# Local attention in six layers: dividing the probabilities before their transposition, and a product with the values that comes out transposed

## The reference

```python
def local_attention(q, k, v):
    ...
    bk2, bv2 = (look(bk), look(bv))      # each window sees the one before and itself: 128 keys
    ...
    sim = jnp.einsum('bhwie,bhwje->bhwij', bq, bk2) * QK_SCALE
    sim = jnp.where(mask, -jnp.finfo(sim.dtype).max, sim)
    attn = jax.nn.softmax(sim, -1)
    out = jnp.einsum('bhwij,bhwje->bhwie', attn, bv2)
    return out.reshape(b, h, n, d)
```

## Time and profile before

| | |
|---|---|
| median of 3 runs | 5177.25 us (5173.41 to 5180.86) |
| profiled execution: span from first to last instruction | 5182.7 us |
| PE busy | 4823.6 us, 93% |
| DVE busy | 3429.4 us, 66% |
| ACT busy | 3112.6 us, 60% |
| POOL busy | 2409.7 us, 46% |
| mean granted TensorE clock | 0.978 |

### The profile page before, as it was taken

How to read it: one execution, slowest core, us unless ns; L and a number is a source line. 1 busy time by engine, 2 the same in 40 slices (tenths; PEclk the granted TensorE clock), 3 DMA queues, 4 the chain that set the end, 5 groups by cost and what they waited for, 6 DMA issues and landing times.

```text
span 5182.7 us, 92467 instructions
## 1 busy us (share of the span) xinstructions
PE 4823.6 (93%) x35414; PEld 3013.7 (58%) x35480; DVE 3429.4 (66%) x6514; ACT 3112.6 (60%) x6618; POOL 2409.7 (46%) x2314
## 2 busy tenths in 40 slices
PE   6898999989899898969999999999999999999998
PEld 2232333334334343227877777777777777777776
DVE  4766566676675857757766666666666666666664
ACT  3565555434344444547777677776777677777763
POOL 3211101111011111129777677676767677776762
PEclk8999999999999899989999999999999999999998
DMA  5233222322312222311000000000000000000000
GB/s 121 52 56 59 54 44 55 65 50 48 61 37 50 46 57 43 56 30 46 8 18 26 16 24 20 22 22 20 22 18 24 18 28 16 24 19 19 24 22 21
DMA packets 125161, 188.97 MB, mean 36 GB/s; under 512 B 18896, under 2 KB 67664, under 8 KB 124496
## 3 DMA queue, kind: packets, MB, share of 16 engines
q1 hardware_dynamic: 124720, 183.06, 15.9%
HBM read 150.09 MB, written 32.51 MB: 35 GB/s over the span
## 4 chain that ended last, share of the span: by engine, by line
PE 64%; DVE 14%; ACT 8%; POOL 7%; issue 6%; DMA 1%; SPq 0%; DVEq 0%; POOLq 0%; ACTq 0%
PE psum L1253 16%; PE psum L1300 10%; PE psum L467 4%; PE psum L432 4%; PE psum L453 4%; DVE maxes L655 3%; PE psum L1308 3%; PE psum L1341 3%; PE psum L1332 2%; PE psum L414 2%; PE psum L1323 2%; POOL stats L1633 2%; PE psum L476 2%; ACT probs L836 2%; PE psum L422 1%
## 5 line engine op out<-in xcount | busy, mean ns | idle before, releaser
L836 ACT ACTIVATE probs<-psum 128x1024 f32<-128x1024 f32 x768 | 772.2, 1019 | 609.9 <-PE psum L453 337.7
L655 DVE TENSOR_REDUCE maxes<-psum 128x1 f32<-128x1024 f32 x512 | 616.5, 1212 | 246.6 <-PE psum L432 242.5
L1633 POOL TENSOR_TENSOR stats<-stats,minus_half 128x8 f32<-128x8 f32 x384 | 651.8, 1697 | 32.0
L1439 DVE TENSOR_TENSOR lwork<-psum,rotary 128x512 f32<-128x512 f32 x384 | 264.2, 688 | 513.1 <-PE psum L1300 446.9
L1573 ACT ACTIVATE lprobs<-psum,small_stats,stats 128x128 f32<-128x128 f32 x1536 | 581.1, 474 | 12.3 <-DVE small_stats L1457 11.5
L1629 POOL TENSOR_TENSOR lwork<-lwork 128x512 f32<-128x512 f32 x384 | 493.9, 1286 | 202.9 <-DVE lwork L1441 202.7
L1300 PE MATMUL psum<-wqkv_hi,xs_hi 128*128 128x512 f32 (+1 forms) x1536 | 554.6, 361 | 33.6 <-POOL xs_lo L1620 17.1
L453 PE MATMUL psum<-stack 98*128 98x512 bf16 x1536 | 513.1, 390 | 72.1 <-DVE maxes L655 32.0
L432 PE MATMUL psum<-stack 96*128 96x512 bf16 x1536 | 473.2, 391 | 64.2 <-ACT probs L836 53.1
L1300 PE MATMUL psum<-wqkv_hi,xs_lo 128*128 128x512 f32 (+1 forms) x1536 | 519.6, 338 | 0.0
L1300 PE MATMUL psum<-wqkv_lo,xs_hi 128*128 128x512 f32 (+1 forms) x1536 | 519.3, 338 | 0.0
(11 more groups left out here) (225 smaller groups left out, 11526.7 us busy)
## 6 DMA issues: line engine op xcount, KB each, us to landing
stack<-k_parts SPq DMA_DIRECT2D x288, 128.0 KB
staged<-in_quads SPq DMA_DIRECT2D x144, 256.0 KB, 3.0
k_parts<-parts SPq DMA_DIRECT2D x48, 384.0 KB, 2.9
stack<-q_parts SPq DMA_DIRECT2D x288, 64.0 KB
staged<-in_w SPq DMA_DIRECT2D x54, 256.0 KB, 2.7
ctx<-in_ctxT SPq DMA_DIRECT2D x24, 512.0 KB, 4.7
q_parts<-parts SPq DMA_DIRECT2D x24, 384.0 KB, 2.3
arena<-in_ctxT SPq DMA_DIRECT2D x8, 512.0 KB, 4.8
```

The source lines that it names most:

```text
L655: ins = vector.tensor_reduce(to, pair(("M", u)), AX.XY, ALU.max)
L836: scalar.activation(probs[:, i % 6, :, :], pair(("E", u)), ACT.Exp).then_inc(S_["E_act"], 1)
L1439: vector.tensor_tensor(v4(t1), v4(qk), bc(rotary[:, d % 2, 0, tt], 2, 4), ALU.mult)
L1633: pool_step(gpsimd.tensor_tensor(st[:, 8:16], st[:, 0:8], minus_half[:, :], ALU.pow))
```

## The change

The probabilities are divided by their sums while queries are still on the partitions, in a new stage `dv`, and the product with the values is made the other way round, so that it comes out with features on the partitions, as the output projection wants it. The stage `ot` and the buffer `heads_out` go.

- ACT's exponentials give their sum over the 128 keys as a second output (`accum_out`).
- `dv` (lag 5): DVE takes the reciprocal of the four sums and multiplies the 128x512 probabilities in place, in SBUF.
- `pt` moves from lag 5 to 6 and waits for `dv`; `pv` from 6 to 7.
- `pv`: the values (128 keys x 64 features of a head) are the stationary side, the transposed probabilities (64 queries) the moving one; two heads share the partitions. ACT copies to `att_hi` and DVE subtracts to `att_lo` straight from that bank.
- `vals`, `mixed_vals` and `lprobs` get one slot more, and lose the column of ones; `mixed_vals` is set to 0 at the start and `vals` no longer set. `x_back` gets no buffer of its own: it lies in the rotary tables' first buffer and its load waits for the last use of that.

```diff
-        for stage, lag in (("qkv", 0), ("rot", 1), ("tr", 3), ("sc", 4), ("ex", 4), ("pt", 5), ("pv", 6), ("ot", 7)):
+        for stage, lag in (("qkv", 0), ("rot", 1), ("tr", 3), ("sc", 4), ("ex", 4), ("dv", 5), ("pt", 6), ("pv", 7)):
...
-    rank = {st: i for i, st in enumerate(("wo", "sc", "tr", "rot", "ot", "pv", "ex", "pt"))}
+    rank = {st: i for i, st in enumerate(("wo", "sc", "tr", "rot", "pv", "dv", "ex", "pt"))}
...
-        vals, mixed = psb("vals", [P, 6, 4, LHD + 1]), psb("mixed_vals", [P, 7, 4, LHD + 1])
+        vals, mixed = psb("vals", [P, 7, 4, LHD]), psb("mixed_vals", [P, 8, 4, LHD])
...
-        probs = psb("lprobs", [P, 2, 4, P])
+        probs = psb("lprobs", [P, 3, 4, P])
...
-        heads_out = psb("heads_out", [P, 2, 4, LHD])
...
-        back = psb("x_back", [P, C, S])
+        back = rotary[:, DEPTH % 2].rearrange("p i t s d -> p (i t s d)").rearrange("p (c n) -> p c n", c=C)
...
                 elif stage == "pt":
-                    PE.wait_ge(S_["ex_act"], at_("ex", u))
+                    PE.wait_ge(S_["dv_dve"], at_("dv", u))
...
-                    for h in range(4):
+                    for pair in range(2):
                         for w in range(2):
-                            ins = tensor.matmul(bank(("pv", u, 0))[64 * w:64 * w + 64, h * (LHD + 1):(h + 1) * (LHD + 1)],
-                                                pt[:, h, 64 * w:64 * w + 64], (va if w else vm)[:, h, :], start=True, stop=True)
+                            for e in range(2):
+                                ins = tensor.matmul(bank(("pv", u, 0))[64 * e:64 * e + 64, pair * P + 64 * w:pair * P + 64 * w + 64],
+                                                    (va if w else vm)[:, 2 * pair + e, :], pt[:, 2 * pair + e, 64 * w:64 * w + 64],
+                                                    start=True, stop=True)
                     ins.then_inc(S_["pv_pe"], 1)
-                elif stage == "ot":
-                    PE.wait_ge(S_["pv_dve"], at_("pv", u))
-                    left(one, ("ot", u, 0), PE)
-                    o = heads_out[:, out_at["o", u][0], :, :].rearrange("p (j e) d -> p j (e d)", j=2)
-                    for pair in range(2):
-                        ins = tensor.transpose(bank(("ot", u, 0))[:, tok(pair)], o[:, pair, :], ident[:, :])
-                    ins.then_inc(S_["ot_pe"], 1)
...
+                elif stage == "dv":
+                    pr, rc = probs[:, prob_at["p", u][0], :, :], soft(u)[:, 8:12]
+                    V.wait_ge(S_["ex_act"], at_("ex", u))
+                    step(vector.reciprocal(rc, soft(u)[:, 0:4]))
+                    step.join()
+                    vector.tensor_tensor(pr, pr, bc(rc, 2, P), ALU.mult).then_inc(S_["dv_dve"], 1)
                 elif stage == "pv":
-                    ps = bank(("pv", u, 0))[:, 0:4 * (LHD + 1)].rearrange("p (h d) -> p h d", h=4)
-                    rc = soft(u)[:, 8:12]
-                    V.wait_ge(S_["pv_pe"], at_("pv", u))
-                    left(out_at, ("o", u), V)
-                    step(vector.reciprocal(rc.rearrange("p (h d) -> p h d", d=1), ps[:, :, LHD:LHD + 1]))
-                    step.join()
-                    vector.tensor_tensor(heads_out[:, out_at["o", u][0], :, :], ps[:, :, 0:LHD], bc(rc, 2, LHD),
-                                         ALU.mult).then_inc(S_["pv_dve"], 1)
-                elif stage == "ot":
                     d, g, b, tt = u
-                    V.wait_ge(S_["ot_act"], at_("ot", u))
-                    vector.tensor_tensor(att_lo[:, :, tok(tt)], wide(bank(("ot", u, 0))[:, 0:2 * P]), att_hi[:, :, tok(tt)].bitcast(F32),
-                                         ALU.subtract).then_inc(S_["ot_dve"], 1)
+                    V.wait_ge(S_["pv_act"], at_("pv", u))
+                    vector.tensor_tensor(att_lo[:, :, tok(tt)], wide(bank(("pv", u, 0))[:, 0:2 * P]), att_hi[:, :, tok(tt)].bitcast(F32),
+                                         ALU.subtract).then_inc(S_["pv_dve"], 1)
...
-                        ins = scalar.activation(pr[:, h, :], scores(u)[:, h % 2, h // 2, :], ACT.Exp, bias=st[:, 4 + h:5 + h], scale=y[:, h:h + 1])
+                        ins = scalar.activation(pr[:, h, :], scores(u)[:, h % 2, h // 2, :], ACT.Exp, bias=st[:, 4 + h:5 + h], scale=y[:, h:h + 1],
+                                                accum_out=st[:, h:h + 1])
...
                 elif stage == "kb":
-                    if u:
+                    if u == 0:
+                        SP.wait_ge(S_["qkv_dve"], at_("qkv", (DEPTH - 2, 0, B - 1, QT - 1)))
+                    else:
                         SP.wait_ge(S_["written"], 16 * C * at_("fin", u - 1))
```

More of the change, by code:

```diff
@@ L1134, in last_part @@
         "xs_act xs_pool lq_dve lq_pool rt_dve qk_pe qkv_pe sq_act qkv_act qkv_dve rot_dve rot_pool tr_pe tr_act sc_pe sc_dve ex_act "
-        "pt_pe pt_act pv_pe pv_dve ot_pe ot_act ot_dve add_pe add_dve fo_pool fa_pe fa_dve fa_act fa_pool fb_pe fb_dve fb_pool fy_pe fy_dve fc_act fc_dve "
+        "dv_dve pt_pe pt_act pv_pe pv_act pv_dve add_pe add_dve fo_pool fa_pe fa_dve fa_act fa_pool fb_pe fb_dve fb_pool fy_pe fy_dve fc_act fc_dve "
         "fgate_pe fh_pe fh_act fg_dve fi_dve fg_pool fw_pe fx_dve band_in rt_in zeroed fin_dve kept_in written").split()}
@@ L1165, in last_part @@
         ln_stats = psb("ln_stats", [P, 2, QT])
-        back = psb("x_back", [P, C, S])
-        ONE = {"qkv": 2, "tr": 1, "pt": 1, "pv": 1, "ot": 1, "wo": 2, "fa": 1, "fb": 1, "fy": 1, "fh": 2, "fw": 1}
-        LEAVES = {"qkv": ("sq_act", "qkv_act"), "tr": ("tr_act",), "pt": ("pt_act",), "pv": ("pv_dve",), "ot": ("ot_dve",), "wo": ("add_dve", "add_dve"),
+        back = rotary[:, DEPTH % 2].rearrange("p i t s d -> p (i t s d)").rearrange("p (c n) -> p c n", c=C)
+        ONE = {"qkv": 2, "tr": 1, "pt": 1, "pv": 1, "wo": 2, "fa": 1, "fb": 1, "fy": 1, "fh": 2, "fw": 1}
+        LEAVES = {"qkv": ("sq_act", "qkv_act"), "tr": ("tr_act",), "pt": ("pt_act",), "pv": ("pv_dve",), "wo": ("add_dve", "add_dve"),
                   "fa": ("fa_dve",), "fb": ("fb_dve",), "fy": ("fy_dve",)}
@@ L1199, in last_part @@
         key_at = use(1, [("tr", 3, [(0,)], ["kT"])], [("sc", 3, [(QT - 1,)], ["kT"], "sc_pe")])
-        val_at = use(6, [("qkv", 4, any_, ["v"])], [("pv", 4, any_, ["v"], "pv_pe")])
-        mix_at = plan(order, range(7),
+        val_at = use(7, [("qkv", 4, any_, ["v"])], [("pv", 4, any_, ["v"], "pv_pe")])
+        mix_at = plan(order, range(8),
                       lambda p: [p[1][:3] + (tt,) for tt in range(QT) if tt == p[1][3] + 1 or tt == p[1][3] == 0] if p[0] == "qkv" else [],
@@ L1212, in last_part @@
         stat_at = use(6, [("qkv", 4, any_, ["norm"])], [("ex", 4, any_, ["norm"], "ex_act")])
-        soft_at = use(4, [("sc", 4, any_, ["soft"])], [("pv", 4, any_, ["soft"], "pv_dve")])
+        soft_at = use(4, [("sc", 4, any_, ["soft"])], [("dv", 4, any_, ["soft"], "dv_dve")])
         stage_at = plan(order, range(2), lambda p: [p] if p[0] == "lq" else [], lambda p: [(p, "lq_pool")] if p[0] == "lq" else [])
@@ L1405, in vector_program @@
             vector.memset(keys[:, :, :, 4 * WIN:5 * WIN], 0.0)
-            vector.memset(mixed[:, :, :, :], 1.0)
-            vector.memset(vals[:, :, :, :], 1.0)
+            vector.memset(mixed[:, :, :, :], 0.0)
             vector.memset(minus_half[:, :], -0.5).then_inc(S_["zeroed"], 1)
@@ L1579, in scalar_program @@
                                       ACT.Copy).then_inc(S_["pt_act"], 1)
-                elif stage == "ot":
+                elif stage == "pv":
                     d, g, b, tt = u
-                    A.wait_ge(S_["ot_pe"], at_("ot", u))
+                    A.wait_ge(S_["pv_pe"], at_("pv", u))
                     if tt == 0 and (d, g, b) != (0, 0, 0):
                         A.wait_ge(S_["add_pe"], order.nth["wo", u[:3]] - 1)
-                    scalar.activation(att_hi[:, :, tok(tt)], wide(bank(("ot", u, 0))[:, 0:2 * P]), ACT.Copy).then_inc(S_["ot_act"], 1)
+                    scalar.activation(att_hi[:, :, tok(tt)], wide(bank(("pv", u, 0))[:, 0:2 * P]), ACT.Copy).then_inc(S_["pv_act"], 1)
                 elif stage == "fq":
```

7 lines of the change are left out of this document (2 added, 5 removed).

## The result

The changed kernel takes 5206.8 us (median of 4, 5203.4 to 5209.1) beside 5178.9 for the kernel before on the same chip. The ratio is 1.0053 [1.0038, 1.0067]: slower by 0.5%, 28 us, where 22 us of gain were forecast. The time lies inside the forecast's range, on the other side of no change.

The account below looks back on a forecast made before the run. TensorE was taken as the bound on average, with ACT already ending last in one turn of seven. The terms sum to -1.8 us a half layer, -22 us over 12, for a forecast of 5155 us, range 5080 to 5235.

Parts of the forecast that it names:

- full: Turns also holding 12 to 36 output-projection or feed-forward matmuls, 16 a half layer: PE's saving kept in 15, -4.65 us.
- with table load: Light turns with ACT's table load ahead of the exponentials, 5 a half layer: PE's saving lost, reads added, +2.35 us.
- behind them: Light turns right behind those with a table load, 3 a half layer: 0.49 us longer each, +1.47 us.
- PE's saving: Two transposes (L1349) go from TensorE: 0.31 us a tile, at most 119 us over 384 tiles.
- Reads: Accumulator reads after ACT's four exponentials: 0.47 us more a tile, bounds 0.36 and 1.25.
- Rival 3: ACT's accumulator read doesn't overlap the short exponentials: 1.25 us a tile, 5297 us, chance 0.12.
- The wait for Square: PE's waits for ACT's Square to empty a bank: mostly gone with five allocations in six, -1.0 us a half layer.
- The multiplication's duration: DVE's 128x512 multiplication in SBUF: 1.0 us, 0.5 more a tile, with levels of 0.69 and over 1.2.
- The multiplication's cost: DVE's longer multiplication on the path: 0.2 us later in turns behind a load turn, some tenths where POOL sets the run.
- The run of three: Three light turns (2737 to 2753) set by POOL, 28.7 of 30 us busy: multiplication meetings cost +0.3 us a half layer.
- The last three: Last three light turns (2761 to 2777): first gains, then ACT and DVE catch up, +0.2 us a half layer.
- rival 2: Multiplication makes DVE the bound once above about 1.1 us on the mean; at 1.99, 5253 us; chance 0.2.

Follow-up runs that it names:

- e3: Changed kernel without ScalarE's sums and without the multiplication (probabilities left undivided): 5095.2 us, 0.9834.
- e5: Changed kernel with one more PSUM bank of the ring given out for dv and left unused, reciprocals still in SBUF: 5229.1 us, 1.0093.
- e2: Changed kernel without the multiplication (reciprocal and accumulator reads stay): 5123.5 us, 0.9886.
- e16: Changed kernel with the multiplication over two of the four heads only (128x256): 5155.8 us, 0.9959.
- e4: Changed kernel with the reciprocals in an extra PSUM bank of the ring, so the multiplication has one SBUF input: 5187.6 us, 1.0014.
- e7: Changed kernel with the multiplication done head by head, as four tensor_scalar of 128x128 with a scalar per partition: 5199.2 us, 1.0038.
- e10: Kernel before, with a one-column Exp right behind the last Gelu to load ScalarE's table early: 5176.3 us, 0.9998.
- e1: Changed kernel without ScalarE's sums (a constant 1 instead), multiplication still run: 5178.9 us, 0.9996.
- e14: Changed kernel with Square later, table loaded early, reciprocals in the product's PSUM bank and att_lo ahead of the multiplication: 5179.7 us, 1.0000.
- e12: Changed kernel with the reciprocals in the product's PSUM bank and ScalarE's table loaded early: 5178.6 us, 1.0000.
- e11: Changed kernel with a one-column Exp right behind the last Gelu to load ScalarE's table early: 5213.0 us, 1.0070.
- e13: Changed kernel with Square moved behind the copies of queries and keys, and ScalarE's table loaded early: 5216.1 us, 1.0074.

## Why the prediction was wrong

The 383 turns between the first and last scores, by the forecast's kinds, in us (sums from the timelines of PE; the forecast's terms times 12, and the Square term apart):

| kind | turns | forecast | measured | without reads and multiplication (e3) |
|---|---|---|---|---|
| full | 183 | -56 | -57.5 | -68.1 |
| with table load | 55 | +28 | +20.6 | +0.4 |
| behind them | 33 | +18 | +26.1 | -11.2 |
| other light | 112 | 0 | +35.5 | -13.3 |

The four kinds make +24.7 us. The first scores start 6.0 us sooner (2326.56, for 2332.55) and the rest behind the last ones is 2.1 longer, which gives the span's 20.8.

- **PE's saving** (0.31 a tile, lost in load turns): right. Full turns got 0.31 each, and e3's load turns show no gain.
- **Reads**: 0.47 a tile forecast, 0.36 measured, the lower bound that the pair in the earlier trace rows gave. Rival 3 (0.31 for each read, 1.25 a tile) falls.
- **The wait for Square**: right, 16.3 to 2.0 us, and by the cause named (five allocations in a ring of six); e5, with six again, has 43.5. This and PE's saving are what the forecast had right in its mechanism.
- **The multiplication's duration**: right, 0.90 for 1.0, with the two levels named.
- **The multiplication's cost: the step that failed.** The forecast let it cost 0.2 us in the three turns behind a load turn and nearly nothing elsewhere, some 13 us in all (0.2 x 3, +0.3, +0.2 a half layer). The whole multiplication costs 84 (against none at all, e2), and what the forecast priced, its growth, at least 51: that is e16 to the changed kernel, and e16's rows of 128x256 are already longer than the old ones. The sum took a mean, 3.89 a turn with 0.44 for the old multiplication, against PE's 4.47, and so saw room. But the turn of 3.89 is one without feed-forward; with it DVE's two turns took 10.02 us, PE's 10.02, and DVE had 0.37 of slack in both together. There a lengthening (0.88 in the first of them) reaches the maximum, the exponentials and the next scores. That stretch was in the trace: from 2559.79 to 2569.81 DVE is unbroken but for 0.37.
- **The run of three** at GpSimd: +0.3 a half layer forecast, +1.6 measured (19.7 us in all). Its last turn went from 6.60 to 9.91, as POOL's rows got longer by 1.3 us (clamp 0.24 to 0.68, two 128x512 from about 1.28 to 1.73) while PE arrived earlier, and as the clock fell behind PE's wait of 2.66 us, worth 1.5. It is so in five half layers (9.8 to 9.9); in those between them the turn went from 5.6 to 6.6. POOL is the bound here (0.5 us idle in 19.4), not DVE (4.4 idle).
- **The last three**: +0.2 a half layer forecast, +1.5 measured (17.7 us in all). e2 has none of it and e4 7.4, so it is the multiplication again; through which wait isn't shown.
- The other light turns as a whole add up to 573.2 us in e4, for 574.0 before and 609.5 after. Without the meetings their loss is gone in sum.
- **The clock** has no term in the forecast, which read 1.00 and kept it. The falls are some 14 us of the result.

So rival 2 was the mechanism in the turns behind a load turn: DVE is the bound there. Its threshold was wrong for the reason above: it was set at a mean of 1.1 us, and 0.90 was enough. In the run of three the multiplication acts through GpSimd, which rival 2 didn't have. That the time fell inside the range is luck: the forecast's own middle had the wrong sign.

Of the 84 us, 41.5 come with the meetings (e4 against e5), the rest with the length, 0.69 where e2 has nothing. On the meetings the Trainium skill, page "SBUF — State Buffer" (Who interferes with whom), is borne out: it says that a DVE instruction with two SBUF inputs contends with a GpSimd one that reads SBUF, by an exclusive lock. Here, with one input in PSUM, the spread is gone (690 ns at most, for 2360). The forecast cited that rule and let a meeting cost DVE its mean; what it costs is decided by what stands behind it, the maximum on DVE or the row that PE waits for on POOL. The cast L1515, which the forecast read as a case of the same sentence, has only one input in SBUF; its long rows (1558 ns at most) are not explained by it.

What stays open: the 6 us ahead of the first scores, of which PE's time at the lower clock (177 of the first 2310 us, for 187) can be up to 5; how much of e7's result is DVE's time and how much POOL's; and what the table load costs when the clock doesn't fall.

## What to carry to other kernels

Before an engine is given more work, find the longest stretch in which it has no gap, not its mean share or its typical turn, and ask what stands behind that stretch in its queue. Here it was a maximum that two other engines needed, on an engine with a busy share of 66%. An instruction that VectorE does out of PSUM is not of the same price in SBUF: keep one operand in PSUM, even four columns of reciprocals, when GpSimd is busy beside it. When an edit shortens one turn and the next takes it all back, the bound is an engine that the edit did not touch; read its rows, which will stand where they stood. And read the granted clock before calling an edit worthless: one that gathers TensorE's idle into a single longer wait can win its microseconds and lose them again at half the clock.

## What the runs showed of the hardware

- The accumulator's read is 0.19 to 0.26 us as a row, but holds the next ACTIVATE back by only 0.09; ACT's busy share counts it in full (336.6 us in all), the path 28.
- A DVE TENSOR_SCALAR of 128x128 with one SBUF tensor and a scalar per partition, 0.27 us at the least, was up to 1.39: all 166 rows over 0.4 us (of 1536, e7) began inside a row of GpSimd. So it isn't only two tensors that meet. A TENSOR_TENSOR with its small operand in PSUM kept to 686 to 690 ns.
- GpSimd suffers as well: its clamp of 128x8 was 389 ns on the mean beside the multiplication in SBUF, and 251 with the reciprocals in PSUM.
- TensorE's granted clock fell from its higher level to its lower (1.2 GHz) for 3.4 us behind waits of 1.75 and 2.66 us in the rows above, and one such fall cost 1.5 us (10.15 for 8.65 in the same turn). Time at the lower level between 2340 us and the last scores: none before, in e4 and in e10; 3 us in e2 and e3, 10 in e16, 20 in e5, 31 in the changed kernel and in e1, 48 in e14, 51 in e12, 82 in e11 and e13.
